# A Mamba block in 64 tiles on one core: weights loaded at the head of a tile, the gate's chain ahead of the exponentials, and the first C.B and gate in other banks

## What is computed

```python
proj = einsum('bsd,ed->bse', x, in_proj_w)        # gate, hs|B|C, dt
hBC  = silu(conv4(proj[hs|B|C]) + conv_b)          # causal, 4 taps, per channel
dt   = clip(softplus(dt + dt_bias), 0, 100)
L    = exp(segsum(dt * A))                         # decay inside a chunk
Y    = (C.B * L) @ (hs * dt)  +  C @ (state of the chunk before) * exp(A_cum)  +  hs * D
g    = Y * silu(gate)
out  = g * rsqrt(mean over the group of g*g + eps) * norm_w @ out_proj_w.T
x = x + out ;  x = x + ffn(layernorm(x))           # ffn: silu(g)*u, block-scaled weights
```

## Time and profile before

| | us |
|---|---|
| median of 3 runs (1875.56 to 1877.73) | 1877.3 |
| the profiled execution, its own time | 1877.94 |
| its span, from the first to the last instruction | 1876.1 |
| PE busy | 1750.3 (93%) |
| DVE busy | 1263.9 (67%) |
| POOL busy | 1184.9 (63%) |
| ACT busy | 840.9 (45%) |

### The profile page before, as it was taken

One profiled execution on the slowest core, in us unless ns is written; L12 is line 12 of the kernel. 1 busy time (PEld: TensorE's weight loads), 2 busy tenths in 40 slices (PEclk: granted clock), 3 DMA queues, 4 the chain that ended last, 5 costly groups with the idle time before them and its releaser, 6 DMA issues. The chain is left out here.

```text
span 1876.1 us, 34372 instructions
## 1 busy us (share of the span) xinstructions
PE 1750.3 (93%) x10392; PEld 1407.7 (75%) x10392; DVE 1263.9 (67%) x1892; ACT 840.9 (45%) x1273; POOL 1184.9 (63%) x873
## 2 busy tenths in 40 slices
PE   6899999999999999999999989999999998999998
PEld 5677787778777877787778777787778776788886
DVE  7777647772787287736874677557854774977776
ACT  4555345543564355535653555345634553322221
POOL 3487658865777568846775588558765777632430
PEclk9899999999999999999999999999999998999999
DMA  2322102210222022202230222012210221111101
GB/s 95 92 64 85 41 29 80 85 46 22 68 80 68 0 79 85 74 0 73 69 94 3 57 80 84 19 51 67 81 40 29 80 75 42 46 57 34 45 23 45
DMA packets 71341, 107.23 MB, mean 57 GB/s; under 512 B 16740, under 2 KB 25060, under 8 KB 71304
## 3 DMA queue, kind: packets, MB, share of 16 engines
q1 hardware_dynamic: 70296, 105.38, 18.8%
q10 hardware_dynamic: 1008, 1.38, 0.2%
HBM read 103.51 MB, written 3.15 MB: 57 GB/s over the span
## 5 line engine op out<-in xcount | busy, mean ns | idle before, releaser
L794 PE MATMUL proj<-xhi,w_hi 128*128 128x512 f32 x1080 | 447.2, 414 | 80.8 <-DVE gate L1116 76.9
L796 PE MATMUL proj<-xhi,w_lo 128*128 128x512 f32 x1080 | 423.7, 392 | 0.0
L795 PE MATMUL proj<-xlo,w_hi 128*128 128x512 f32 x1080 | 423.6, 392 | 0.0
L794 PEld LDWEIGHTS proj<-xhi,w_hi 128*128 128x128 f32 x1080 | 203.1, 188 | 174.7 <-DVE gate L1116 101.7
L1097 DVE SCALAR_TENSOR_TENSOR v<-proj,par_sb,v 128x510 f32<-128x510 f32 x378 | 279.9, 742 | 72.5 <-ACT v L590 51.7
L492 POOL TENSOR_TENSOR g_lo<-gated,g_hi 128x512 fp32r<-128x512 f32 x128 | 164.0, 1284 | 198.4 <-ACT g_hi L723 198.3
L427 POOL TENSOR_TENSOR w_lo<-w_raw,w_hi 128x512 fp32r<-128x512 f32 x144 | 182.5, 1286 | 138.0 <-ACT w_hi L568 138.0
L796 PEld LDWEIGHTS proj<-xhi,w_lo 128*128 128x128 f32 x1080 | 203.3, 188 | 45.0
L795 PEld LDWEIGHTS proj<-xlo,w_hi 128*128 128x128 f32 x1080 | 203.8, 189 | 35.7
L467 POOL TENSOR_TENSOR gated<-hs,gate 128x512 f32 (+1 forms) x128 | 190.0, 1506 | 51.0 <-DVE hs L1222 51.0
L590 ACT ACTIVATE v<-proj,par_sb 128x512 f32<-128x512 f32 x126 | 97.8, 776 | 248.4 <-PE proj L796 248.4
(11 more groups left out here) (164 smaller groups left out, 3360.4 us busy)
## 6 DMA issues: line engine op xcount, KB each, us to landing
w_raw<-in_win SPq DMA_DIRECT2D x144, 256.0 KB, 4.2
fade_l<-faded SPq DMA_DIRECT2D x128, 256.0 KB, 3.7
wo_raw<-in_wout SPq DMA_DIRECT2D x64, 256.0 KB, 2.6
M<-in_w SPq DMA_DIRECT2D x14, 512.0 KB, 3.8
row_r<-rows SPq DMA_DIRECT2D x256, 3.0 KB
row_l<-rows SPq DMA_DIRECT2D x256, 3.0 KB
cb<-in_w SPq DMA_DIRECT2D x7, 512.0 KB, 3.3
out<-resid SPq DMA_DIRECT2D x8, 256.0 KB, 2.0
```

What stands on the lines that cost most here:

```text
L794: e.matmul(o, hi_l, hi_r, start=first, stop=False)
L795: e.matmul(o, hi_l, lo_r, start=False, stop=False)
L796: return e.matmul(o, lo_l, hi_r, start=False, stop=last)
```

## The change

In a step: SP issues `load_pair` first, no longer last. ACT scales `wo_raw` before the first tap of half 1 and casts it before the tanh of hs half 0; `gate_tanh` of half 0 comes before `exponential` of z = 0, no longer after. DVE runs `gate_silu` of half 0 before both `weigh_own`; `hs_silu` of half 0 goes after the second of half 1's three convolution steps, no longer after the first. PE's order in a step is as it was.

In the set-up: `cbs` runs before the last two units and writes the two `proj` banks and `misc`, and the two gate units write the y banks, once ACT has read the sums out of them. ACT copies the sums before the tanh of C's half 1. DVE keeps C.B before the silu products of the first hs. In the windows `cbs` keeps its banks. PE waits for `taken` 8 before the first step.

The core of the diff (the set-up's changed bank arguments on ACT and DVE are left out):

```diff
             def step(g, j, par_, nxt, nxt2, ahead):
+                if nxt2:
+                    load_pair(9 * g + j + 3, split.at(g, j, 0))
                 sp.wait_ge(wolo.sem, wolo.at(g, j, 0))
...
-                if nxt2:
-                    load_pair(9 * g + j + 3, split.at(g, j, 0))
...
             hs_tanh(bc[:, 1, :], 0, 3)
-            hs_tanh(bc[:, 1, :], 1, 4)
             act.wait_ge(s_cum, 1)
...
             e.copy(parts[:, 0, :], acum).then_inc(s_part[0], 1)
+            hs_tanh(bc[:, 1, :], 1, 4)
...
                 if ahead:
                     bounded(g, j + 1, 1)
-                    exponential(g, j + 1, 0)
                 if nxt:
                     gate_tanh(gate[:, 1 - par_, :], 0, ready.at(g, j, 3))
                 if ahead:
+                    exponential(g, j + 1, 0)
                     exponential(g, j + 1, 1)
...
-            for n in range(CUM_AFTER + 1, 8):
-                first_unit(n)
...
-            pe.wait_ge(taken.sem, 6)
+            pe.wait_ge(taken.sem, 4)
             pe.wait_ge(s_fade_s, 1)
-            cbs(4)
+            cbs(4, *proj)
             pe.wait_ge(s_cumread, 2)
             pe.wait_ge(s_fade_l, 2)
+            for n in range(CUM_AFTER + 1, 8):
+                first_unit(n)
+            pe.wait_ge(taken.sem, 6)
...
-                    if d <= len(between):
-                        between[d - 1]()
+                    if d == 2 and between:
+                        between()
...
                     hs_silu(hs[:, 1 - par_, :], 1, tanh.at(g, j, 2))
+                    gate_silu(gate[:, 1 - par_, :], 0, tanh.at(g, j, 3))
                 if ahead:
                     weigh_own(g, j + 1, 0)
-                if nxt:
-                    gate_silu(gate[:, 1 - par_, :], 0, tanh.at(g, j, 3))
-                if ahead:
                     weigh_own(g, j + 1, 1)
```

More of the change, by code:

```diff
@@ L601, in hs_tanh, with gate_tanh @@
                 e.activation(halves(dst, h), v[:, h, :], ACT.Tanh).then_inc(tanh.sem, 1)
-            def gate_tanh(dst, h, nready):
+            def gate_tanh(dst, h, nready, banks=proj):
                 act.wait_ge(ready.sem, nready)
-                e.activation(halves(dst, h), proj[h][:, :], ACT.Tanh, scale=0.5).then_inc(tanh.sem, 1)
+                e.activation(halves(dst, h), banks[h][:, :], ACT.Tanh, scale=0.5).then_inc(tanh.sem, 1)
             act.wait_ge(s_dtv, 2)
@@ L644, in _ @@
             upper_pair(1, 2)
-            gate_tanh(gate[:, 0, :], 0, 7)
-            gate_tanh(gate[:, 0, :], 1, 8)
+            gate_tanh(gate[:, 0, :], 0, 7, ybank)
+            gate_tanh(gate[:, 0, :], 1, 8, ybank)
             def bc_tile(g, i, r0, k0, s0):
@@ L682, in step @@
                     upper_pair(par_, 9 * g + j + 3)
-                if nxt:
-                    tap3(1, w, ready.at(g, j, 2), silu.at(g, j, 0))
-                    act.wait_ge(gdone.sem, gdone.at(g, j, 0))
-                    hs_tanh(hs[:, 1 - par_, :], 0, taken.at(g, j, 1))
                 act.wait_ge(woraw.sem, woraw.at(g, j, 16))
@@ L691, in step @@
                     .then_inc(woscaled.sem, 1)
+                if nxt:
+                    tap3(1, w, ready.at(g, j, 2), silu.at(g, j, 0))
                 act.wait_ge(woscaled.sem, woscaled.at(g, j, 1))
@@ L843, in first_unit @@
                 pair, piece, h = n // 4, (n // 2) % 2, n % 2
-                free = (None, None, None, None, 1, 2, 3, 4)[n]
-                project(1 - pair, piece, h, 2 * pair + piece + 1, free, (diff, proj)[piece])
+                free = (None, None, None, None, 1, 2, None, None)[n]
+                project(1 - pair, piece, h, 2 * pair + piece + 1, free, ((diff, proj), (diff, ybank))[pair][piece])
             dt_turned = (trb, misc)
@@ L902, in _ @@
             exponents(0, 0, 0)
+            pe.wait_ge(taken.sem, 8)
             def step(g, j, par_, nxt, nxt2, ahead):
@@ L979, in window @@
                         pe.wait_ge(rdone.sem, rdone.window(g, 1))
-                        cbs(silu.window(g, 4))
+                        cbs(silu.window(g, 4), *diff)
                     if not nxt and kk and t >= 2:
@@ L1088, in _, with conv_rest @@
             e.tensor_scalar(parbc_sb[:, :, :, :], parbc_sb[:, :, :, :], 0.5, None, ALU.mult).then_inc(s_halved, 1)
-            def conv_rest(h, weights, ntap, nconv, between=(), banks=proj):
+            def conv_rest(h, weights, ntap, nconv, between=None, banks=proj):
                 dve.wait_ge(tap.sem, ntap)
@@ L1161, in _, with cbs_kept @@
             conv_rest(1, w, 6, 10, banks=diff)
-            for h in range(2):
-                hs_silu(hs[:, 0, :], h, h + 5)
-            def cbs_kept(ncb):
+            def cbs_kept(ncb, banks):
                 dve.wait_ge(cbr.sem, ncb)
                 mask = upto[:, :].unsqueeze(1).broadcast_to([P, B, P])
-                for kind, src in enumerate((diff[0], diff[1], misc)):
+                for kind, src in enumerate((banks[0], banks[1], misc)):
                     if kind == 1:
@@ L1175, in cbs_kept @@
                     ins.then_inc(cbd.sem, 1)
-            cbs_kept(1)
-            gate_silu(gate[:, 0, :], 0, 7)
-            gate_silu(gate[:, 0, :], 1, 8)
+            cbs_kept(1, proj)
+            for h in range(2):
+                hs_silu(hs[:, 0, :], h, h + 5)
+            gate_silu(gate[:, 0, :], 0, 7, ybank)
+            gate_silu(gate[:, 0, :], 1, 8, ybank)
             dve.wait_ge(s_fade_s, 1)
@@ L1216, in step @@
                     conv_rest(1, w, tap.at(g, j, 2), convs.at(g, j, 2),
-                              (lambda: hs_silu(hs[:, 1 - par_, :], 0, tanh.at(g, j, 1)),))
+                              lambda: hs_silu(hs[:, 1 - par_, :], 0, tanh.at(g, j, 1)))
                 own = tile_weights(t)
@@ L1252, in window @@
                     if t == 3 and nxt:
-                        cbs_kept(cbr.window(g, 1))
+                        cbs_kept(cbr.window(g, 1), diff)
                     if not nxt:
```

14 lines of the change are left out of this document (8 added, 6 removed).

## The result

The changed kernel takes **1773.24 us** (median; 1772.93 to 1773.83) against 1876.71 for the kernel before, measured alongside: ratio 0.9449, 95% interval 0.9433 to 0.9466. The profiled execution took 1772.93 for a span of 1771.1. The forecast was 1769, its own range 1761 to 1782.

What follows compares the result with a forecast made beforehand. DVE's chain was taken to hold PE, whose own 15.12 us a tile then bounds. Steady tiles 89.3, first intervals 7.4 and transitions 8.2 make 104.9; with set-up 3.5, 1877.94 falls to 1769.5, median 1769, range 1761 to 1782.

Steps and rivals of the forecast that it cites:

- What bounds the kernel: Steady tile: PE waits on DVE's chain to the gate; 17.17 us now, PE's own 15.12 becomes the bound, 2.05 to give.
- The ring: Experiments' theory, not forecast: L1222, `gated`, `weigh_past`, fade loads, `w_raw` load, casts, tap, convolution, next L1222; 17.19 us around.
- The gate's order: Gate half 0 ahead of DVE's weighings and ACT's exponentials: PE starts at 119.15, not 120.28; alone 1.13 us a tile.
- Rival B: Half the effect: second tap stays late, only the gate order helps, 1.13 a tile, 53 us; 1813 us; chance 0.07.
- Weights ahead: `w_raw` load first in SyncE's step: ACT's 3.00 wait and DVE's 0.85 idling go, with 0.08 of start overlap.
- hs_silu one step later: DVE's `hs` half 0 after the second convolution step, not the first: 0.16 us of step latency comes back.
- The tie: `hs` half 0 arrives at 7.04, POOL's `wo_lo` starts at 6.98; one or two slow tiles a group, 0.15 us mean.
- Transitions: Each group's last tile: two smaller waits, before `unit(3)` and the window's first unit, fall; 1.2 x 7 = 8.2 us.
- Set-up: C.B to `proj`, first gate to `ybank`, sums copied ahead of a tanh: +3.5 us, bounds +4.5 and -4.8.
- A: Port convoy: every tile's `hs` half 0 meets a fresh POOL operation, 15.80 a tile; 1794 us; chance 0.14.
- C: The kernel gets slower, its sign PEclk under 1.00 inside the groups; no time given; chance 0.03.
- D: Something else waits at the same place (the load's wait holds SyncE's queue), nothing changes: 1877 us; chance 0.02.

Runs made afterwards that it cites:

- ACT's old order: Changed kernel with ACT's three moved operations put back (tap of half 1, tanh of hs half 0, then scaling and cast of `wo_raw`): 1762.95 us, ratio 0.9375.
- place 1: `hs_silu` of half 0 after the first of half 1's convolution steps: 1797.88 us in the changed kernel, 1796.8 us with ACT's old order.
- the last experiment: The 1762.95 us kernel (ACT's old order) with the set-up's first two `hs_silu` ahead of keeping C.B: 1762.88 us, ratio 0.9387.
- place 3: Changed kernel with `hs_silu` of half 0 after the third of half 1's convolution steps, not the second: 1788.1 us, ratio 0.951.
- place 2: `hs_silu` of half 0 after the second of half 1's convolution steps, as in the changed kernel itself: 1773.24 us, ratio 0.9449.
- the kernel with `wo_lo` late: Changed kernel with POOL's `wo_lo` moved behind `gated`: 1774.12 us, ratio 0.9436.

## Why the prediction was right, and where not

**What bounds the kernel.** Right in its result, wrong in its reading. PE's own 15.12 a tile is the bound after: 15.11 is measured. But "the question is how much DVE's chain lets go" read the wait before `unit(0)` as the cause of 17.17. The ring above was the cause; the wait for the gate was where its time became visible. That the number held all the same is the bound's doing: with every part in place a tile stands at PE's 15.12, whichever link was taken for the cause.

**The gate's order.** The step that failed is "Alone this lets PE start at 118.49 + 0.62 + 0.06 = 119.15, not 120.28: 1.13 us" (the sum is 119.17, so 1.11). PE does start earlier, and alone that brings 0.0 us of 1877, since it then waits for `v`. Rival B rested on the same 1.13 (53 us in the tiles) and was wrong with it. With the load early the order brings 47 us, almost 1.0 a tile. So of the two edits the load was the one that had to come first: 70 us alone, and 132 as the last one to be added (1905.06 - 1773.24).

**Weights ahead.** The effect was forecast, and its signs are there: ACT's wait for `w_raw` falls from 171.8 us in 58 to one of 3.0; DVE's for `v` from 85.6 in 69 to 31.0 in 14; L1225 starts 8.15 after the turn where the sum gave 8.25 (and 8.2 was the low end of what was to be seen). The reason why it mattered was half seen: I had the 3.00 of ACT and what it delays, and did not follow the load back to the `weigh_past` that held it, and from there to L1222.

**hs_silu one step later.** Mis-sized: I charged it 0.16 of latency. In fact the place is worth 24.6 us in the changed kernel and 33.9 with ACT's old order. My own frame held the answer: with place 1 DVE would come at 7.04 - 0.67 = 6.37, inside the split that ends at 6.98.

**The tie.** Right in mechanism and size: one tile of each group, 0.52 to 0.70 over, where one or two were expected; the mean of the 47 is 15.21 against 15.27, the term 91.5 against 89.3. The drift shows in `hs_silu`'s own lengths from tile to tile of the first group: 0.68, 0.78, 1.69, 1.13, 0.82, 0.89, 0.68 and 1.71. The Trainium skill ("SBUF — State Buffer", section "Who interferes with whom") says that a DVE instruction with two SBUF inputs and a GpSimd instruction that reads SBUF exclude each other for a whole instruction, and that DVE with at most one SBUF input does not take part. The rows agree with both: `hs_silu` behind `wo_lo` above, and `gate` from the PSUM bank y at 63.18, 0.69 long in the middle of a `weigh_past` of 2.40 that started at 62.76. What the loser needs after the lock is measured as 0.54 to 0.55 and not its full 0.69.

**Transitions.** Mis-sized: 0.53 each and not 1.2. The two waits of a group's last tile were said to fall; but that tile is where the drift arrives at the tie a second time (the 1.71 above, L1225 9.11 after its turn), and PE waits again. With the tie gone (ACT's old order) a transition is 75.14 and the gain 1.15, so the 1.2 was right for a kernel without it.

**Set-up.** Mis-sized: 1.9 of 3.5, inside its bounds, and the first turn does not come the 3 to 4 us earlier that were to be seen. The first matmul of `unit(0)`, before and then after:

```profile
67.21 0.79 PE L794 MATMUL proj<-xhi,w_hi 128*128 128x512 f32 x1
```

```profile
67.77 0.49 PE L795 MATMUL proj<-xhi,w_hi 128*128 128x512 f32 x1 [2.18 <-DVE gate L1119]
```

From there to the turn it took 5.29 (to 72.50) and takes 2.85 (to 70.62): the full clock brought 2.44. But it starts 0.56 later, after C.B at 0.54 of the clock and three products held up by POOL. Two of these three are worth no more than the 0.5 that the last experiment shows; how the rest divides was not measured. The wait of 2.18 is for both gate products (`taken` 8), which read the y banks; `proj0`, which `unit(0)` writes, was free once C.B had been kept at 61.70. Whether a wait placed behind `unit(0)` would bring the time was not tried.

**The rivals.** A was right as a mechanism for place 1 (15.72 measured for 15.80), in weaker form for place 3 (15.51), and wrong for place 2, the one in the change. C: PE was busy 128.50 of 129.00 us from 71 to 200 at a granted clock of 1.00; nothing of it happened, nor of D, which the 70 us of the load alone rule out.

The sum gave 3.4 us of span too much: 4.5 of the transitions and 1.6 of the set-up were not there, and the tiles, first intervals and the rest gave 2.7 more. The forecast lay 4 us low.

## What to carry to other kernels

Before an edit is costed at a wait, follow the waiting chain once round a full period, through the DMA queue too: if it closes on itself, only what lies on the ring is worth anything, and it may be cut at more than one link (here 70 us at SP and 53 us at ACT, against 0 for the gate, which is not on it). An operation that two engines dispute is best placed where the other one waits for something else; a pause of about 1 us on POOL gained 10 us. And of several edits made together, measure the change without each of them: one part was worth 0 alone and 47 in company, and the whole without the load was slower than where it started.

## What the runs showed of the hardware

- A DVE product of two SBUF operands (128 x 512, 0.69 alone) that arrives during a POOL instruction that reads SBUF ends 0.53 to 0.56 after it: so in each of the 190 rows of `hs_silu` over 1.3 us that could be paired in the changed kernel, its places 1 (both) and 3 and the kernel with `wo_lo` late. In the other order POOL's subtraction goes from 1.29 to 1.76, so the loss goes to whoever is second by as little as 0.14 us.
- The lock is by the instruction, not by the group of two that the profile puts in one row: in the kernel with `wo_lo` late, `hs_silu` waited only for the second half of the split.
- After PE's wait of 4.82 us the granted clock was 0.54 from 55 to 60, under C.B, and 1.00 from 60 on; between tiles, with pauses of up to 0.4 us, it stayed at 1.00. So it did in the kernel before, with pauses of up to 1.56 in nearly every tile (1.00 over 200 to 1440).
- What stays open: between the last gate product of the set-up and the first matmul of `unit(0)` lie 0.7 us in three kernels, where the tiles show 0.06. The product of `fade_s` behind the gate ends about 0.1 before that matmul, but only DVE waits for its semaphore in the kernel; PE waits there for `taken` 8, ahead of the loop of steps. What fills the 0.7 is not shown.
